# Another order for the last two front steps and for the middle steps of a two-layer vision tower

## The chip, the cores and the metric

The kernel runs on one core of a Trainium2 chip. The metric is device time in microseconds, from one launch to its end; the median of several runs counts. The engines are TensorE (PE in the profile, its weight loads PEld), VectorE (DVE), ScalarE (ACT), GpSimd (POOL) and SyncE (SP). They run side by side, each with its own queue in order, and wait for each other by semaphores. An engine also waits for its own earlier instruction by a semaphore where it reads that one's result.

## The reference

128 images are cut into 64 patches each, embedded, given a class token and multiplied by a positional table: 128 x 65 tokens of width 128. Two layers follow. L0 has attention (softmax over the queries) and 32 experts with a ReLU, two per token, gated by sigmoids; L1 mixes tokens by a decaying sum whose size is scaled by a norm, and has 16 experts with a GELU and four times the width, two per token, gated by softmax values.

```python
    h = _L0_tok_ref(x, ...)
    h = h + _L0_attn_ref(_layernorm(h, axis=-1), ...)
    h = h + _L0_ffn_ref(_layernorm(h, axis=-1), ...)
    h = h + _L1_attn_ref(_layernorm(h, axis=-1), L1_attn_k)
    h = h + _L1_ffn_ref(_layernorm(h, axis=-1), ...)
```

## The kernel before

**Front.** 16 groups of 8 images (520 tokens, five tiles of 104 rows). Each group is embedded, goes through attention (stages a1 to a4: token-major copy and norm, transposes, queries and keys, values and scores, softmax; b1 and b2: product with the values, sum h1T, transposes back to token-major htok), and is routed to the experts (r1 to r3). For each token and each of its two experts, a row of 132 numbers (the normalized token, place, gate, spread, mean) is scattered to the expert's list in HBM: POOL issues ten indirect DMAs per group (send). Where a row goes (slots) is the expert's base plus the token's rank there; the ranks come from one-hot rows (oh, ohs) by matmuls on PE (r3) and a running count.

A step works on the routing of group g and the attention of group g + 1. The last two steps, late_step on PE and ACT and a list of calls on DVE, belong to groups 14 and 15. There the router works on the sums h1T ahead of the norm (late_r2, with selC, the centred expert matrix), since the order of the logits doesn't change by the norm's scale: late_choice takes the two best, late_experts finds their indices and one-hots, late_added sums them, late_rows computes the norm's power (three dependent Newton instructions), the scaled logits eg, and writes the first copy of the rows; ACT copies them for the second expert (r1_rows1) and takes the exponential of eg; late_gate and late_slots end it. For group 15 the softmax and the product with the values are done in two halves of four images (last_a4 and last_b1 on DVE, last_b1 on PE).

**Tables and blocks of L0.** tables(L0) on DVE and PE computes from the counts which expert each block of 256 rows belongs to. Its first value, t_fr, says where each list ends; SP and ACT wait for it and write rows of padding there. 73 blocks follow: load the expert's weights and rows (SP, ACT), transpose, two matmuls with a ReLU between them, scale by the gate, scatter the results (POOL, two indirect DMAs a block). The first eight blocks are loaded before, from the groups that are known; the others wait for all rows and the padding.

**Middle.** 13 groups of 640 tokens. For each, two results per token are added (gather on DVE, line L2139), normed, mixed by two banded products on PE (delta, context), added to the tokens (mixed_in, L2178), normed, routed and sent (POOL, ten indirect DMAs a group; the send's issue is line L2316, that of the results L2344). Groups 0 and 1 lie among L0's blocks; groups 2 to 12 are steps of their own, mid_step on PE, ACT and DVE. Rows and slots have three buffers: group g may write its rows when the send of group g - 3 has landed (scattered). The names of the row buffers are rows (two of them) and w_emb (groups 2, 5, 8, 11).

**Blocks of L1** are like L0's, with four times the width; the results are added up and stored.

The order on each engine is written out by hand: a function per engine lists the calls, and a wait on one engine holds up all that stands behind it there. SP has no part in the change; POOL's queue is the sends and results in their order, unchanged.

## Time and profile before

| | |
|---|---|
| median of 3 runs | 1103.01 us (1102.77 to 1104.39) |
| profiled execution, its own time | 1099.68 us |
| its span, from the first to the last instruction | 1097.9 us |
| busy in the span: PE, DVE | 913.5 us (83%), 861.2 us (78%) |
| busy in the span: POOL, ACT | 676.5 us (62%), 498.8 us (45%) |
| front until L0's first table value | 448 us |
| L0's blocks, with groups 0 and 1 of the middle among them | to about 677 us |
| middle groups 2 to 12, and L1's tables | to about 816 us |
| L1's blocks and the sums | to the end |

The shares are means over stages that have different limits; what a change is worth is read in its stage.

### The profile page before, as it was taken

How to read it: one execution, taken by the hardware profiler on the slowest of the kernel's cores; microseconds unless marked ns; L12 is line 12 of the kernel's file. 1: busy time of each engine (PE TensorE's matmuls, PEld its weight loads, DVE VectorE, ACT ScalarE, POOL GpSimd, SP SyncE). 2: the span in 40 equal slices, each digit the busy share in tenths (PEclk: the TensorE clock that was granted, in tenths of full speed). 3: DMA queues.
4: the chain of work that ended last, by engine and by line, in shares of the span. 5: the costliest groups of instructions: out<-in, count | busy, mean ns of one | idle time of the engine just before them, and what ended most of it. 6: DMA issues, size and time to landing. Idle time of an engine off the chain costs nothing.

```text
span 1097.9 us, 21730 instructions
## 1 busy us (share of the span) xinstructions
PE 913.5 (83%) x6064; PEld 773.1 (70%) x6064; DVE 861.2 (78%) x3321; ACT 498.8 (45%) x1338; POOL 676.5 (62%) x622
## 2 busy tenths in 40 slices
PE   6999999999999996476775877767549999999992
PEld 2576666777766665366665866766549999999992
DVE  1488989888888986666686898998767777888883
ACT  1355555555544442111111554666525555655651
POOL 1026666767766646677677667777777555555553
PEclk9999999999999996678788887777759999999996
DMA  9955666555666204477779964665295888979886
GB/s 371 358 201 206 214 225 219 197 200 201 218 223 213 72 22 139 127 212 207 205 225 312 299 228 150 232 211 168 76 330 169 294 271 288 296 261 333 303 275 232
DMA packets 118664, 246.57 MB, mean 225 GB/s; under 512 B 20914, under 2 KB 85936, under 8 KB 112400
## 3 DMA queue, kind: packets, MB, share of 16 engines
q1 hardware_dynamic: 77440, 191.26, 51.5%
q0 software_dynamic: 18592, 34.68, 9.3%
q10 hardware_dynamic: 22512, 19.25, 5.8%
q8 instruction: 48, 0.79, 0.3%
q14 instruction: 72, 0.59, 0.2%
HBM read 201.68 MB, written 45.43 MB: 225 GB/s over the span
## 4 chain that ended last, share of the span: by engine, by line
PE 38%; DVE 25%; issue 11%; DMA 9%; SPq 7%; ACT 5%; POOL 3%; ACTq 1%; DVEq 0%; POOLq 0%
PE ps L1002 8%; PE ps L980 5%; DMA xin<-lists_L 4%; PE ps L753 3%; PE ps L820 3%; DMA results_L<-xin 3%; PE ps L804 2%; SPq L607 2%; POOL lists_L L2316 2%; SPq L609 2%; SPq L600 2%; ACT x_hi L1180 2%; PE ps L792 2%; PE ps L746 2%; DVE idx L1686 2%
## 5 line engine op out<-in xcount | busy, mean ns | idle before, releaser
L2316 POOL DMA_INDIRECT lists_L<-rows,slots x250 | 282.3, 1129 | 164.1 <-issue 156.1
L2344 POOL DMA_INDIRECT results_L<-xin x145 | 145.8, 1005 | 105.3 <-DVE xin L2116 73.7
L2344 POOL DMA_INDIRECT results_L<-xin,place x146 | 143.7, 984 | 59.7 <-issue 38.9
L753 PE MATMUL ps<-xin,w_emb 128*128 128x512 f32 x292 | 137.4, 607 | 10.1 <-DMA w_emb<-in_w_main 8.2
L1002 PE MATMUL ps<-xin,QK 128*128 128x128 f32 x838 | 115.6, 289 | 1.8 <-DVE xin L2116 1.7
L1002 PEld LDWEIGHTS ps<-xin,QK 128*128 128x128 f32 x838 | 108.2, 205 | 3.1 <-issue 3.0
L1364 ACT ACTIVATE QK<-ps,xin 128x256 f32<-128x256 f32 x164 | 64.2, 474 | 82.0 <-PE ps L980 82.0
L2325 POOL TENSOR_TENSOR x_lo<-xin,x_hi 128x2048 fp32r<-128x2048 f32 x13 | 60.1, 4626 | 63.3 <-ACT x_hi L1188 63.0
L957 PE MATMUL ps<-ident,xin 128*128 128x128 f32 x291 | 66.5, 311 | 36.0 <-DMA xin<-lists_L 33.8
L753 PEld LDWEIGHTS ps<-xin,w_emb 128*128 128x128 f32 x292 | 52.8, 194 | 58.8 <-issue 47.8
L2090 DVE TENSOR_SCALAR xin<-xin 128x128 f32<-128x128 f32 x291 | 92.9, 364 | 0.6
L1002 PE MATMUL ps<-xin,UH 128*128 128x128 f32 x648 | 89.1, 283 | 2.6 <-DVE xin L2116 2.4
L1207 ACT ACTIVATE h0T<-ps 128x256 f32<-128x256 f32 x73 | 27.8, 382 | 131.4 <-PE ps L957 100.7
L1002 PEld LDWEIGHTS ps<-xin,UH 128*128 128x128 f32 x648 | 81.4, 197 | 4.3 <-issue 4.3
L980 PE MATMUL ps<-x_hi,x_lo 128*128 128x256 f32 x256 | 78.6, 307 | 1.1 <-DVE x_lo L2084 1.1
L975 PE MATMUL ps<-h0T,xin 128*128 128x128 f32 (+1 forms) x326 | 59.5, 319 | 19.1 <-ACT h0T L1207 8.8
L980 PE MATMUL ps<-x_hi 128*128 128x256 f32 x256 | 73.1, 285 | 0.0
L980 PE MATMUL ps<-x_lo,x_hi 128*128 128x256 f32 x256 | 73.0, 285 | 0.0
L957 PEld LDWEIGHTS ps<-ident,xin 128*128 128x128 f32 x291 | 39.4, 158 | 43.8 <-DMA xin<-lists_L 41.3
L1364 ACT ACTIVATE UH<-ps,xin 128x256 f32<-128x256 f32 (+1 forms) x160 | 55.4, 429 | 31.1 <-PE ps L980 29.3
L975 PEld LDWEIGHTS ps<-h0T,xin 128*128 128x128 f32 x326 | 53.7, 237 | 21.7 <-ACT h0T L1207 11.2
L2105 DVE TENSOR_TENSOR xin<-ps,xin 128x256 f32<-128x256 f32 x81 | 32.1, 397 | 44.3 <-PE ps L1002 44.2
(347 smaller groups left out, 2418.8 us busy)
## 6 DMA issues: line engine op xcount, KB each, us to landing
xin<-in_x_main SPq DMA_DIRECT2D x48, 1536.0 KB, 6.7
xin<-in_w_L SPq DMA_DIRECT2D x81, 578.0 KB
xin<-in_w_L SPq DMA_DIRECT2D x98, 128.0 KB
xin<-lists_L SPq DMA_DIRECT2D x64, 132.0 KB
xin<-in_w_L ACTq DMA_DIRECT2D x65, 128.0 KB
x_hi<-results_L SPq DMA_DIRECT2D x13, 640.0 KB, 6.3
xin<-in_difference SPq DMA_DIRECT2D x13, 640.0 KB, 4.6
xin<-in_distance SPq DMA_DIRECT2D x13, 640.0 KB
```

What stands on the lines that cost most here:

```text
L753: mm = pe.matmul(psE[h], w_emb[:, k, :], xin[h][c][:, n, :], start=(k == 0), stop=False, skip_group_check=True)
L820: mm = pe.matmul(pair[2][:, c:c + SEQ], V[h][:, i, :], Pr[h][:, i, :], start=True, stop=True)
L957: mm = pe.transpose(ps[:, banks(l, i)[0], q * 128:(q + 1) * 128], xblk[b][:, q, 0:D], ident[:, :])
L975: mm = pe.matmul(bank_h(i, f)[:, of_part], w1, xTb[p2][:, of_part], start=True, stop=True)
L980: mm = pe.matmul(bank_h(i, f)[:, 0:n_in], w[p2][:, cols_f], x[p2][:, 0:n_in], start=(n2 == 0), stop=(n2 == 2), skip_group_check=True)
L1002: mm = pe.matmul(o, hTb[p2][:, f, rows_in], w2[:, f * D:(f + 1) * D], start=(f == 0), stop=(f == l.FC - 1))
L1364: ins = act.activation(hTb[p2][:, f, 0:n_in], ps[:, 2 + 2 * p2 + f // 2, f % 2 * l.block:f % 2 * l.block + n_in], ACT.Gelu, bias=b1)
L2090: ins = dve.tensor_scalar(xblk[u][:, q, 0:D], xblk[u][:, q, 0:D], xblk[u][:, q, SPREAD:SPREAD + 1], xblk[u][:, q, MEAN:MEAN + 1], ALU.mult ...
L2105: dve.tensor_tensor(yblk[u][:, 0:Q, :], y, wblk[u][:, None, l.W - D:l.W].to_broadcast([128, Q, D]), ALU.add)\
L2316: pool.indirect_dma_start(out=lists[l.name], out_offset=bass.IndirectOffsetOnAxis(ap=slots_of(l, g, h)[:, t, k:k + 1], axis=0), in_=buf[:, ...
L2325: pool.tensor_tensor(x_lo0[:, :, :].rearrange("p k n -> p (k n)"), xin[h][0][:, 0:KS, :].rearrange("p k n -> p (k n)"), x_hi0[:, :, :].rea ...
L2344: pool.indirect_dma_start(out=results[l.name], out_offset=bass.IndirectOffsetOnAxis(ap=where, axis=0), in_=yblk[u][:, q, :], in_offset=Non ...
```

## The change

In the last two front steps: ACT copies the transposed tokens of group 15 ahead of the guess for group 14's norm. PE computes the scores ahead of the values (last_a4 on PE), and DVE takes the scores (a3) ahead of the ranks and of the copy of the values, with the slots of group 14 between the two halves of the softmax. For group 15 PE transposes the sums (last_b2) ahead of the router (late_r2); DVE takes the statistics first, computes the power before the experts' indices, and no longer writes rows: ACT writes both copies from htok with a scale and a shift (last_rows; last_shift on DVE gives the shift). late_rows is split into late_power and late_rows, late_slots into late_pick and late_slots.

In the middle steps DVE's functions are written anew so that instructions that don't depend on each other alternate: the Newton steps of the next group's norm stand among the one-hots (newton_half, newton_off, newton_power), those of the mixing among the rows (mid_rows), the slots of the group before behind the first tile of the rows (mid_slots), the mean and variance of the next group between the logits and their maxima. ACT normalizes the next tokens before it copies the rows, and takes the gate's exponentials before the decays. The instructions are the same ones as before, but for the order and two additional waits.

```diff
+            def last_a4(g, h):
+
+                pe.wait_ge(q_ready, g + 1)
+                pe.wait_ge(k_ready, g + 1)
+                for i in range(GI):
+                    c = i // 4 * BANK + i % 4 * SEQ
+                    mm = pe.matmul(pair[1][0:SEQ, c:c + SEQ], KTt[:, i * SEQ:(i + 1) * SEQ],
+                                   QT[:, i * SEQ:(i + 1) * SEQ], start=True, stop=True)
+                mm.then_inc(s_ps, 1)
+                for i in range(GI):
+                    mm = pe.matmul(pair[0][0:SEQ, i * D:(i + 1) * D], x1T[h][:, i * SEQ:(i + 1) * SEQ], wv[:, :],
+                                   start=True, stop=True)
+                mm.then_inc(v_ps, 1)
+
+            def last_b2(g):
+
+                pe.wait_ge(h1T_ready, g + 1)
+                for t in range(TILES):
+                    if t == 2:
+                        pe.wait_ge(h1T_ready, g + 2)
+                    mm = pe.transpose(pair[2][0:ROWS, t * 128:(t + 1) * 128], h1T[:, t * ROWS:(t + 1) * ROWS], ident[:, :])
+                mm.then_inc(hT_ps, 1)
+
             def late_r2(g):
 
                 pe.wait_ge(h1T_ready, g + 1)
                 pe.wait_ge(consts_dve, 3)
                 for t in range(TILES):
-                    if t == 2 and g + 1 == GROUPS:
-                        pe.wait_ge(h1T_ready, g + 2)
                     mm = pe.matmul(late_logit[:, t, :], h1T[:, t * ROWS:(t + 1) * ROWS], selC[:, :], start=True, stop=True)
                 mm.then_inc(S["L0"].lg_ps, 1)
 
...
                 if g + 1 < GROUPS:
                     b1(g, h, j)
                     a1(g + 1, 1 - h, j + h)
+                    late_r2(g)
+                    b2(g, h, j)
                 else:
                     last_b1(g, h)
-                late_r2(g)
-                b2(g, h, j)
+                    last_b2(g)
+                    late_r2(g)
                 if g + 1 < GROUPS:
                     a2(g + 1, 1 - h, j + h)
                     a3(g + 1, 1 - h, j + h)
                 r3(L0, g, h, j)
                 if g + 1 < GROUPS:
-                    a4(g + 1, 1 - h, j + h)
+                    last_a4(g + 1, 1 - h)
 
...
+            def last_rows(g, h, j):
+
+                s, ln, buf = S["L0"], second["L0"], rows_of(L0, g, h)
+                act.wait_ge(s.top_ready, g + 1)
+                act.wait_ge(s.scattered[h], 16 * TILES * TOP * j)
+                for t in range(TILES):
+                    ins = act.activation(buf[:, t, :, 0:D], htok[h][:, t, None, :].to_broadcast([ROWS, TOP, D]), ACT.Identity,
+                                         scale=ln.rs[:, t:t + 1], bias=ln.shift[:, t:t + 1])
+                ins.then_inc(s.rows1_ready, 1)
+
...
@@ -1314,14 +1347,17 @@
                     a1(g + 1, o, jo)
                     guess(LNA, g + 1, statsA, logA, guessA)
                 b2(g, h, j)
+                if g + 1 < GROUPS:
+                    a2(g + 1, o, jo)
                 guessB(L0, g)
                 if g + 1 < GROUPS:
-                    a2(g + 1, o, jo)
                     a3(g + 1, o, jo)
                 late_r2(g)
-                r1_rows1(L0, g, h, j)
                 if g + 1 < GROUPS:
+                    r1_rows1(L0, g, h, j)
                     a4(g + 1, o, jo)
+                else:
+                    last_rows(g, h, j)
 
...
                     absolute(g + 1)
+                if 0 <= g + 2 < MG:
+                    normalized(g + 2)
                 if g >= 0:
                     r1_rows1(L1, g, g % 2, g // 2)
-                if 0 <= g + 2 < MG:
-                    normalized(g + 2)
                 if 0 <= g + 1 < MG:
                     guessB(L1, g + 1)
+                if g >= 0:
+                    r2(L1, g, g % 2, g // 2)
                 if 0 <= g + 2 < MG:
                     decays(g + 2)
-                if g >= 0:
-                    r2(L1, g, g % 2, g // 2)
                 if 0 <= g + 2 < MG:
...
-            def last_a4(g, h):
-
-                st = Steps(NA * g + 4)
...
+            def last_a4(g, h, n):
+
+                st, i = last_steps, slice(n * GI // 2, (n + 1) * GI // 2)
+                dve.wait_ge(exp_ready, g + 2 + n)
...
+                dve.tensor_tensor(Pr[h][:, i, :], Pr[h][:, i, :], ssum[:, i, None].to_broadcast([SEQ, GI // 2, SEQ]),
+                                  ALU.mult).then_inc(p_ready, 1)
+
+            last_steps = Steps(NA * (GROUPS - 1) + 4)
 
...
-            def late_rows(g, h, j):
-
-                s, w, ln, buf = S["L0"], W["L0"], second["L0"], rows_of(L0, g, h)
+            def late_power(g):
+
+                s, w, ln = S["L0"], W["L0"], second["L0"]
                 dve.wait_ge(s.guessB, g + 1)
                 dve.scalar_tensor_tensor(ln.half[:, 0, :], ln.guess[:, 0, :], -0.5, ln.guess[:, 0, :],
                                          ALU.mult, ALU.mult).then_inc(s.dveR, F.one())
@@ -1931,10 +1967,23 @@
                 dve.scalar_tensor_tensor(ln.rs, ln.off[:, 0, :], 1.5, ln.guess[:, 0, :],
                                          ALU.add, ALU.mult).then_inc(s.dveR, F.one())
                 dve.wait_ge(s.dveR, F.all())
+                if g + 1 == GROUPS:
+                    last_shift()
                 dve.tensor_tensor(w.eg[:, :, :], w.top8[:, :, 0:TOP], ln.rs[:, :, None].to_broadcast([L0.rows, TILES, TOP]),
                                   ALU.mult).then_inc(s.top_ready, 1)
+
+            def last_shift():
+
+                ln = second["L0"]
+                dve.wait_ge(S["L0"].dveR, F.all())
+                dve.scalar_tensor_tensor(ln.shift[:, :], ln.mv[:, :, 0], -1.0, ln.rs, ALU.mult, ALU.mult)
+
+            def late_rows(g, h, j):
+
+                s, ln, buf = S["L0"], second["L0"], rows_of(L0, g, h)
                 dve.wait_ge(s.scattered[h], 16 * TILES * TOP * j)
-                norm_apply(ln, htok[h], lambda t: buf[:, t, 0, 0:D]).then_inc(s.rows0_ready, 1)
+                if g + 1 < GROUPS:
+                    norm_apply(ln, htok[h], lambda t: buf[:, t, 0, 0:D]).then_inc(s.rows0_ready, 1)
                 dve.tensor_copy(buf[:, :, 0, MEAN], ln.mv[:, :, 0])
                 dve.scalar_tensor_tensor(buf[:, :, 0, SPREAD], ln.mv[:, :, 1], EPS, ln.rs, ALU.add, ALU.mult)\
                     .then_inc(s.spread_ready, 1)
...
-            def late_slots(g, h, j):
+            def late_pick(g):
 
                 s, w, p, E = S["L0"], W["L0"], L0.rows, L0.E
                 dve.wait_ge(s.rank_ps, g + 1)
@@ -1961,6 +2010,10 @@
                 dve.wait_ge(s.dveR, marks["added"])
                 dve.tensor_tensor(counted(L0, g + 1), counted(L0, g), w.added[:, 0:E], ALU.add).then_inc(s.dveR, F.one())
                 marks["counted"] = F.all()
+
+            def late_slots(g, h, j):
+
+                s, w, p, E = S["L0"], W["L0"], L0.rows, L0.E
                 dve.wait_ge(s.rank_read, g + 1)
...
             late_experts(g)
             r1(L0, g, h, j)
             late_added(g)
+            late_power(g)
             late_rows(g, h, j)
             late_gate(g, h)
+            a3(g + 1, 1, j)
+            late_pick(g)
+            a2(g + 1, 1, j)
+            last_a4(g + 1, 1, 0)
             late_slots(g, h, j)
-            a2(g + 1, 1, j)
-            a3(g + 1, 1, j)
-            last_a4(g + 1, 1)
+            last_a4(g + 1, 1, 1)
             g, h = 2 * j + 1, 1
             last_b1(g, h)
+            r1(L0, g, h, j)
             late_choice(g)
+            late_power(g)
             late_experts(g)
-            r1(L0, g, h, j)
+            late_rows(g, h, j)
             late_added(g)
+            late_gate(g, h)
+            late_pick(g)
             late_slots(g, h, j)
-            late_rows(g, h, j)
-            late_gate(g, h)
 
...
+            def mid_slots(g):
+                s, w = S["L1"], W["L1"]
+                dve.wait_ge(s.dveR, marks["rank"])
+                dve.scalar_tensor_tensor(slots_of(L1, g, g % 2)[:, :, :], w.idx8[:, :, 0:TOP], float(L1.room),
+                                         w.rank[:, :, :], ALU.mult, ALU.add).then_inc(s.slot_ready, 1)
+
+            def mid_rows(g):
+
+                s, ln, x, buf = S["L1"], second["L1"], m_tok[g % 2], rows_of(L1, g, g % 2)
+                norm, magnitude, turn = one_of(g + 2), one_of(g + 1), g + 3
+                which = slice(0 if norm is not None else 1, 2 if magnitude is not None else 1)
+                dve.wait_ge(s.dveR, marks["power"])
+                dve.wait_ge(s.scattered[g % 3], 16 * TILES * TOP * (g // 3))
+                for t in range(TILES):
+                    ins = dve.tensor_scalar(buf[:, t, 0, 0:D], x[:, t, :], ln.mv[:, t, 0:1], ln.rs[:, t:t + 1],
+                                            ALU.subtract, ALU.mult)
+                    if t == 0 and g > LAST + 1:
+                        mid_slots(g - 1)
+                    if t == 2 and magnitude is not None:
+                        dve.wait_ge(m_guess, turn)
+                        dve.scalar_tensor_tensor(LNC.half[:, which, :], LNC.guess[:, which, :], -0.5,
+                                                 LNC.guess[:, which, :], ALU.mult, ALU.mult).then_inc(dveM, sm.one())
+                    if t == 3 and magnitude is not None:
+                        dve.wait_ge(dveM, sm.all())
+                        dve.scalar_tensor_tensor(LNC.off[:, which, :], LNC.base[:, which, :], TINY,
+                                                 LNC.half[:, which, :], ALU.add, ALU.mult).then_inc(dveM, sm.one())
+                ins.then_inc(s.rows0_ready, 1)
+                if magnitude is not None:
+                    dve.wait_ge(dveM, sm.all())
+                    if norm is not None:
+                        dve.wait_ge(m_ntok, norm)
+                    dve.wait_ge(actx_ready, magnitude)
+                    dve.scalar_tensor_tensor(LNC.power[:, which, :], LNC.off[:, which, :], 1.5,
+                                             LNC.guess[:, which, :], ALU.add, ALU.mult).then_inc(dveM, sm.one())
+                dve.tensor_copy(buf[:, :, 0, MEAN], ln.mv[:, :, 0])
+                dve.scalar_tensor_tensor(buf[:, :, 0, SPREAD], ln.mv[:, :, 1], EPS, ln.rs, ALU.add, ALU.mult)\
+                    .then_inc(s.spread_ready, 1)
+                if magnitude is not None:
+                    dve.wait_ge(dveM, sm.all())
+                    if norm is not None:
+                        dve.scalar_tensor_tensor(LNC.shift[:, :], LNC.mv[:, :, 0], -1.0, LNC.rs, ALU.mult, ALU.mult)
+                    dve.tensor_tensor(mag, ssq, LNC.power[:, 1, :], ALU.mult).then_inc(m_powers, 1)
+                dve.tensor_copy(buf[:, :, :, PLACE].bitcast(I32),
+                                places["L1"][:, g:g + 1, :].rearrange("p o (t k) -> p (o t) k", t=TILES))\
+                    .then_inc(s.place_ready, 1)
+
+            def mid_tokens(g):
+
+                s, ln = S["L1"], second["L1"]
+                if g + 3 < MG:
+                    h = (g + 3) % 2
+                    dve.wait_ge(m_in[h], 16 * ((g + 3) // 2 + 1))
+                    h2 = h2tok[(g + 3) % 3]
+                    dve.tensor_tensor(h2[:, :, :], yin[h][:, :, 0, :], yin[h][:, :, 1, :], ALU.add).then_inc(m_free[h], 1)
...
+                if g + 1 < MG:
+                    mixed_in(g + 1)
...
+                if g + 1 < MG:
+                    dve.wait_ge(s.htok_ready, g + 2)
+                    for t in range(TILES):
+                        ins = dve.bn_stats(ln.bn[:, t, :], m_tok[(g + 1) % 2][:, t, :])
+                    ins.then_inc(s.statsB_step, 1)
...
+            def mid_ranked(g):
+
+                s, w, E, p = S["L1"], W["L1"], L1.E, L1.rows
+                if g + 1 < MG:
+                    newton_half(g + 1)
...
             def mid_step(g):
 
-                h, j = g % 2, g // 2
-                r1_apply(L1, g, h, j)
+                mid_rows(g)
                 if g == L1.known + 1:
                     first_table(L1)
-                if g < MG - 1:
-                    powers(one_of(g + 2), one_of(g + 1), g + 3)
-                if g + 3 < MG:
-                    gather(g + 3)
-                if g + 1 < MG:
-                    mixed_in(g + 1)
-                    r1(L1, g + 1, 1 - h, (g + 1) // 2)
+                mid_tokens(g)
                 if g == L1.known:
                     first_counts(L1)
-                st = r2(L1, g, h, j)
-                r2_gate(L1, g, h, j, st)
...
+                mid_chosen(g)
+                mid_ranked(g)
...
+            for f in (newton_half, newton_off, newton_power):
+                f(LAST + 1)
             for g in range(LAST + 1, MG):
                 mid_step(g)
+            mid_slots(MG - 1)
+            dve.wait_ge(S["L1"].slot_ready, MG)
             tables(L1)
```

mid_chosen is r2's part up to the indices, and mid_ranked the rest of r2, r2_gate, r3 and r3_slots, in the alternating order; newton_half, newton_off and newton_power are newton's three instructions.

## Rows read from the trace of the kernel before

**Rows 1.** DVE's timeline, 425 to 448: start us, us, engine, line, operation, output<-inputs.
```profile
429.78 0.75 DVE L1606 SCALAR_TENSOR_TENSOR Sm<-ps,causal 65x260 f32<-65x260 f32 x2
430.56 0.69 DVE L1610 TENSOR_REDUCE smax<-Sm 65x8 f32<-65x520 f32 x1
...
434.54 0.42 DVE L1865 TENSOR_TENSOR Pr<-Pr,ssum 65x260 f32<-65x260 f32 x1
...
437.50 0.43 DVE L1880 TENSOR_TENSOR UH<-UH,ps 128x260 f32<-128x260 f32 x1 [1.18 <-PE ps L854]
439.27 0.33 DVE L1887 COPY lg<-ps 104x160 f32<-104x160 f32 x1 [1.34 <-PE ps L865]
...
442.02 0.24 DVE L1911 TENSOR_TENSOR ohs<-oh 104x160 bf16<-104x160 bf16 x1
...
443.38 0.45 DVE L1553 BATCH_NORM_AGGREGATE mvB<-bnB 104x2 f32<-104x6 f32 x5
...
445.14 0.17 DVE L1973 SCALAR_TENSOR_TENSOR slots<-idx,rank 104x10 uint32<-104x10 uint32 x1
...
446.04 1.36 DVE L1558 TENSOR_SCALAR rows<-htok,mvB,powerB 104x128 f32<-104x128 f32 x5
...
447.87 0.12 DVE L1782 SCALAR_TENSOR_TENSOR t_fr<-iotaB,ps 1x32 int32<-1x32 f32 x1
```

**Rows 2.** POOL's timeline, 440 to 452; in brackets the idle time before.
```profile
449.07 0.99 POOL L2316 DMA_INDIRECT lists_L<-rows,slots  x1 [6.15 <-ACT rows L1207]
```

**Rows 3.** Chain of waits, 395 to 650: start us, us, what.
```profile
464.83 2.06 DMA lists_L<-padrows
```

**Rows 4.** DVE's timeline, 680 to 700: slots of group 2.
```profile
682.97 0.17 DVE L1739 SCALAR_TENSOR_TENSOR slots<-idx,rank 128x10 uint32<-128x10 uint32 x1
```

**Rows 5.** POOL's timeline, 684 to 838, first issue of group 2 and first result of L1.
```profile
690.95 0.96 POOL L2316 DMA_INDIRECT lists_L<-w_emb,slots  x1 [0.30 <-issue]
...
832.45 0.99 POOL L2344 DMA_INDIRECT results_L<-xin  x1 [0.30 <-issue]
```

**Rows 6.** Busy time by stretches; columns: PE, PEld, DVE, ACT, POOL busy, PEclk, DMA, GB/s.
```profile
815.00:822.00 7.00, 5.92 (x32) 5.46 (x28) 3.65 (x11) 1.75 (x5) 5.43 (x6) 0.50 0.94 290
...
846.00:1098.00 252.00, 227.87 (x1983) 226.48 (x1983) 190.31 (x533) 134.87 (x347) 135.07 (x135) 0.97 0.83 282
```

**Rows 7.** PE's timeline, 844 to 847.
```profile
846.68 0.33 PE L957 MATMUL ps<-ident,xin 128*128 128x128 f32 x1 [1.58 <-DMA xin<-lists_L]
```

**Rows 8.** PE's timeline, 412 to 448.
```profile
418.09 1.13 PE L777 MATMUL ps<-ident,ntok 104*128 104x104 f32 x5 [2.00 <-DVE ntok L1558]
422.40 2.10 PE L792 MATMUL ps<-XT,small 128*128 128x260 f32 x4 [3.18 <-ACT XT L1207]
...
426.36 1.91 PE L804 MATMUL ps<-small,XT 128*65 128x128 f32 x16
428.11 1.11 PE L810 MATMUL ps<-QK 128*65 128x65 f32 x16
433.82 3.65 PE L854 MATMUL ps<-Pr,V 65*128 65x65 f32 x16 [4.60 <-DVE Pr L1865]
```

**Rows 9.** ACT's timeline, 412 to 448.
```profile
421.76 0.58 ACT L1207 ACTIVATE XT<-ps 128x520 f32<-128x520 f32 x1
...
440.37 0.70 ACT L1207 ACTIVATE htok<-ps 104x640 f32<-104x640 f32 x1 [6.32 <-PE ps L770]
```

**Rows 10.** DVE's timeline, 795 to 811: rows of group 12, L1's first table value.
```profile
798.96 1.37 DVE L1558 TENSOR_SCALAR rows<-htok,mvD,powerD 128x128 f32<-128x128 f32 x5
...
809.95 0.16 DVE L1782 SCALAR_TENSOR_TENSOR t_fr<-iotaB,ps 1x16 int32<-1x16 f32 x1 [0.51 <-PE ps L894]
```

**Rows 11.** POOL's timeline, 584 to 796: first and last of the delayed issues.
```profile
587.02 1.17 POOL L2344 DMA_INDIRECT results_L<-xin,place  x1 [0.30 <-issue]
...
791.73 1.38 POOL L2316 DMA_INDIRECT lists_L<-rows,slots  x1 [0.30 <-issue]
```

**Rows 12.** DVE's timeline, 784 to 796: the add at the last of them.
```profile
791.45 0.83 DVE L2178 TENSOR_TENSOR htok<-atok,xin 128x640 f32<-128x640 f32 x1 [1.46 <-ACT xin L1437]
```

121 lines of the change are left out of this document (107 added, 14 removed).

## The prediction

> **What bounds the kernel now.** I first read the page's busy time by slices against the stretches of the program, then the chain of waits over the change's first place (400 to 470 us), then the timelines of VectorE (DVE), ScalarE (ACT), TensorE (PE) and GpSimd (POOL) there, and last POOL's timeline through the middle. The reader is to see three stages with different limits.
>
> At the end of the front (groups 14 and 15) almost nothing overlaps: the chain hops PE, ACT, DVE, PE. It ends in the first table value t_fr at 447.87 and in the sends of group 15 at 449.07 [rows 1, 2]. Everything behind hangs on t_fr: the pad rows that ACT and SP write after it have landed at 466.9 [rows 3], and the loads of the ninth block on wait for them.
>
> In the middle (groups 2 to 12 of L1) the chain of waits names DVE for every step up to 798, and DVE has hardly a gap. I don't follow it there. The tile names on POOL's issues tell which group is being sent, since groups 2, 5, 8, 11 send from w_emb. The slots of group 2 are ready at 683.14, but its first issue is at 690.95, and POOL goes from there to the first L1 result at 832.45 with gaps of 0.30 only [rows 4, 5]: 110 issues in 141.5 us, 1.286 each. POOL is always behind DVE and sets the end of the middle; the releaser "DVE slots" that the trace prints is a coincidence of times.
>
> In L1's blocks PE is busy 228 of 252 us [rows 6]. Their start is one wait: PE had finished what it could and sat 1.58 us until a token load landed at 846.68 [rows 7]. That load waits for a result scatter, which stands behind POOL's last send.
>
> **The change part by part.** *ACT's copy of x1T ahead of guessB (step 14).* The transposes end at 419.22 (418.09 + 1.13), the copy began at 421.76 because the guess stood before it [rows 8, 9]. It can start at 419.3: 2.5 us earlier. The guess waits for statistics that come only after that, so putting it second costs nothing; were they early, it would be late by the copy, 0.58.
>
> *Scores before values, DVE's a3 before pick and copy of V.* q and k (from 419.9 in place of 422.40) end at 423.7, k's copy at 424.4; then the scores, 1.11 as before or up to twice that if the clock is low, to 425.5 to 426.1. Sm and smax take 1.47 (429.78 to 431.25), so smax ends at 427.6 instead of 431.25: 3.65 earlier [rows 1, 8]. From there ACT's eight exponentials end after 2.8; DVE has pick, V's copy, the first half of the probabilities and the rest of the slots in that time, 3.5 in all, and then the second half: 4.4 from smax to the end of Pr against 3.7 before (431.25 to 434.96). Gain left 2.95. The product with V starts on the first half: its 3.65 [rows 8] run from 430.3 with little wait between the halves, to 433.95, and h1T ends at 434.4 instead of 437.93 [rows 1]: **3.5 us**. What it costs: slots of group 14 come 2.4 later, so POOL's ten sends end at 445.2 and not at 442.92; POOL sat idle 6.15 us there [rows 2], so 3.9 of idle time is left as cover, and group 15 can go at 445.2.
>
> *Transposes before the router, rows of group 15 by ACT.* Before, h1T to t_fr was 9.94 (437.93 to 447.87). After: three transposes that wait for the second half 0.7 (five take 1.13 at 418.09), htok's copy 0.70, statistics 1.57 (442.26 to 443.83); the router's result is there by then (behind the transposes' new wait stand only the router and the ranks, which need the same half). Logits to ohs 2.99 (439.27 to 442.26); between them the power and eg 0.73 (445.31 to 446.04) and one new small instruction, shift, 0.2; copies and gate 0.47 (447.40 to 447.87); added, pick, slots 1.48 (443.83 to 445.31); then PE's counts, which lay under the rows before and are now a wait, 0.51 as in the other table [rows 1, 8, 9, 10]. Sum 9.35; I add 0.2 for waits: **0.4 us**. The row writing of 1.36 leaves DVE. On ACT it is five instructions of 2x128 columns; the trace has no such shape; by the 0.70 for 640 columns [rows 9] they take between 1.4 (columns alone) and 3.5 (five whole ones); I take 2. DVE's 4 us from eg to the last slot hides either; without that cover the difference would be added to POOL's start only.
>
> So t_fr comes 3.9 earlier, group 15's sends 3.9 earlier. The pads, tables and blocks of L0 follow by the same instructions, and POOL's unbroken run (which begins in L0's last blocks) with them. **-3.9 us**, bounds -2.0 (PE at the low clock through V's product, so that everything from V's copy comes late) and -4.7.
>
> *Middle steps.* The Newton links, means and slots are set between independent instructions; DVE's step gets shorter. I cost this at **nothing**: POOL's issues hide it, and the third row buffer stops DVE when it runs ahead. Rows of group 12 were written at 798.96; they need group 9's send, whose last issue ended at 793.11 [rows 10, 11], so DVE can gain less than 5.8 there, and I take 3.5. If POOL were not the bound, the saving would be about 1.5 per step. Slots now wait behind the next group's buffer wait; two sends earlier must have landed, while POOL has a whole send of 12.9 us left: no starvation.
>
> *POOL against DVE.* An add of two 640-column tiles (L2139, L2178) that is running when an issue starts delays it: the add of 791.45 to 792.28 made the issue at 791.73 last 1.38 and not 0.97 [rows 11, 12]. In the steady steps each add starts just after an issue has begun, and none costs. Where steps are uneven (thirteen adds, from the issue at 587.02 to the one at 791.73) five issues lost 0.08 to 0.41, 1.18 in all, 0.09 per add [rows 11]. The new order breaks the steady places. Eighteen adds are in groups 2 to 11; two cost 0.55 before. Bounds: 0 and 18 x 0.41 = 7.4 in place of 0.55. I take the drifting rate: 1.6, **+1.1 us**.
> The Trainium skill (SBUF — State Buffer, section "Who interferes with whom") says that a VectorE instruction with two SBUF inputs contends with a GpSimd instruction that reads SBUF, and that the second to issue fully blocks; these rows agree. The same section holds that descriptor generation is not stalled by a tensor_tensor; by that the term would be 0 and the sum -3.9, but the 1.38 speaks against it.
>
> *PE's wait before 846.68.* L1's tables come 3.5 earlier than POOL's end, so PE's 1.58 us wait grows to about 5. That alone costs nothing, for the load sets the restart. But after the idle time before 815 PE ran 7 us at half of the full clock by its granted clock of 0.50 [rows 6]; the same here would add up to 3.5. PE works between two shorter waits, so I take 0, and keep 3.5.
>
> Sum: -3.9 + 0 + 1.1 + 0 = -2.8. The profiled execution took 1099.68 (span 1097.9, 1.8 around it), 3.3 below the median of the runs, 1103.01; against it 1096.9, against the median **1100.2 us**. Below, times are against the median.
>
> **Rivals.**
> *Given back (no change).* The front gains, but POOL's delays come to 2 to 5 us more, or PE restarts at half clock, or V's product meets the low clock: 1101 to 1105. For it: POOL has no slack from 650 to 832, so each delay counts whole; against: five of thirteen drifting adds cost anything.
> *Slower: port collisions alone.* The new order puts each add across the start of an issue, and keeps it there, since DVE is held by POOL's landings and so keeps step with it. At 0.41 for 18 adds, 7.4 less 0.55 is +6.9, net +3.0: 1106.0. It decides from 0.36 per add (6.0 + 0.55 over 18). For it: the place copy and the first add now stand side by side; against: no stretch of the trace shows more than one such delay in a step.
> *The chain is right about DVE.* Then nine steps give 1.5 each, 13.5, and with the front 17: about 1086. Against it stands the 7.8 us between slots and issue of group 2.
> *The front does nothing*, because pads and loads end by another wait: 1103. Against: the pads start from t_fr.
>
> **How the numbers follow.** About 0.2% (2.2 us) is what a measurement can tell. Forecast (front kept, POOL pays little): 0.46; given back: 0.35; a front that does nothing: 0.03; slower: 0.12; DVE the bound: 0.04. Faster 0.50, same 0.38, slower 0.12. The range reaches from the full front with no delays and some luck in PE's clock, -6.5, to the middle of the slower case, +1.5: 1096.5 to 1104.5; the likeliest case alone is 1098.3 to 1100.8.
>
> **What would show it.** In the new profile: x1T's copy right after its transposes; smax about 3.6 earlier; t_fr and group 15's first send near 444 and 445; five ACT instructions after eg that nothing waits for; the first mid send and the first L1 result earlier by the same 4, less long issues between; DVE with gaps in the middle; PE idle around 5 us before L1's ninth block. It is wrong if POOL has gaps in the middle (then DVE counted), if many issues last 1.2 or more (collisions), or if t_fr moves by less than 2.

## The result and the profile after

The changed kernel takes 1096.92 us (median of 4 runs, 1092.84 to 1098.53) against 1103.70 for the kernel before (4 runs, 1102.77 to 1104.83): 6.8 us less, a ratio of 0.9933 (95% interval 0.9903 to 0.9962). I had forecast 1100.2, range 1096.5 to 1104.5: the direction is right, the gain more than twice as large as its sum of 2.8. The profiled execution took 1092.84, span 1091.1; the pair of profiled executions also differs by 6.84.

VectorE's timeline of the kernel after, 424 to 445, for [rows 1] (start us, us, engine, line, operation, output<-inputs, idle time before):

```profile
425.47 0.76 DVE L1642 SCALAR_TENSOR_TENSOR Sm<-ps,causal 65x260 f32<-65x260 f32 x2 [0.76 <-PE ps L852]
426.27 0.69 DVE L1646 TENSOR_REDUCE smax<-Sm 65x8 f32<-65x520 f32 x1
...
427.44 1.21 DVE L1632 TENSOR_TENSOR V<-ps,per_row 65x1024 f32<-65x1024 f32 x1
...
429.83 0.17 DVE L2026 SCALAR_TENSOR_TENSOR slots<-idx,rank 104x10 uint32<-104x10 uint32 x1
...
430.44 0.42 DVE L1899 TENSOR_TENSOR Pr<-Pr,ssum 65x260 f32<-65x260 f32 x1
...
432.93 0.42 DVE L1916 TENSOR_TENSOR UH<-UH,ps 128x260 f32<-128x260 f32 x1 [0.99 <-PE ps L868]
435.06 1.06 DVE L1584 BATCH_NORM_STATS2 bnB<-htok 104x6 f32<-104x128 f32 x5 [1.71 <-ACT htok L1230]
...
442.28 0.17 DVE L2026 SCALAR_TENSOR_TENSOR slots<-idx,rank 104x10 uint32<-104x10 uint32 x1
442.97 0.18 DVE L1818 SCALAR_TENSOR_TENSOR t_fr<-iotaB,ps 1x32 int32<-1x32 f32 x1 [0.52 <-PE ps L915]
```

smax (the scores' maxima, for the softmax) ends at 426.96 and not at 431.25, the second half of the probabilities at 430.86 (434.96), h1T at 433.35 (437.93), and t_fr starts at 442.97 (447.87): 4.9 earlier. Three smaller groups of the same kernel: TensorE's timeline [rows 8], ScalarE's [rows 9], POOL's [rows 2].

```profile
424.31 1.13 PE L852 MATMUL ps<-QK 128*65 128x65 f32 x16 [0.24 <-ACT QK L1264]
425.27 1.91 PE L856 MATMUL ps<-small,XT 128*65 128x128 f32 x16
```

```profile
418.94 0.60 ACT L1230 ACTIVATE XT<-ps 128x520 f32<-128x520 f32 x1 [2.35 <-PE ps L777]
...
438.64 2.55 ACT L1334 ACTIVATE rows<-htok,shiftB,powerB 104x256 f32<-104x256 f32 x5
```

```profile
444.33 0.99 POOL L2543 DMA_INDIRECT lists_L<-rows,slots  x1 [0.30 <-issue]
...
686.38 0.97 POOL L2543 DMA_INDIRECT lists_L<-w_emb,slots  x1 [0.30 <-issue]
...
742.65 1.36 POOL L2543 DMA_INDIRECT lists_L<-rows,slots  x1 [0.30 <-issue]
...
827.63 0.99 POOL L2571 DMA_INDIRECT results_L<-xin  x1 [0.30 <-issue]
```

Behind t_fr the last pads go out 4.8 earlier too, by the chain of waits [rows 3]:

```profile
460.04 1.98 DMA lists_L<-padrows
```

ACT's copy of x1T follows its transposes; the five instructions for the rows take 2.55, and nothing waits for them. Group 15's first send comes 4.74 earlier and now directly behind group 14's ten. In the middle POOL is what it was: from group 2's first issue to the first result of L1 141.25, against 141.50 [rows 5], with no gap but its 0.30. So the first result of L1 comes 4.82 earlier, the last one 6.80 (1075.48 against 1082.28).

VectorE's waits of the kernel after, 690 to 800 (line, what it waited for: us in total, times, longest):

```profile
DVE halfC L2287 <- ACT guessC L1457: 7.2, 7, 1.5
DVE lg L2346 <- PE ps L838: 4.3, 1, 4.3
DVE pick L2407 <- PE ps L903: 3.7, 6, 0.8
DVE rows L2281 <- DMA lists_L<-rows,slots: 3.5, 3, 2.5
```

The new order did shorten VectorE's step (busy 78.3 of the 100 us from 695 to 795; before, 87.6), and the time came back as waits, among them the one for a row buffer to come free (the last line). TensorE begins L1's blocks at 807.18, and stands still twice, each time until a token load has landed:

```profile
835.54 0.44 PE L978 MATMUL ps<-ident,xin 128*128 128x128 f32 x2 [2.14 <-DMA xin<-lists_L]
...
840.98 0.33 PE L978 MATMUL ps<-ident,xin 128*128 128x128 f32 x1 [1.78 <-DMA xin<-lists_L]
```

These 3.92 in place of 1.58 [rows 7] cost nothing by the clock. Busy time by stretches (columns as in [rows 6]): 0.57 granted at the start of L1's blocks, 1.00 around those waits.

```profile
807.20:814.20 7.00, 5.92 (x32) 5.52 (x31) 3.66 (x11) 1.85 (x5) 5.37 (x6) 0.57 1.06 358
...
830.00:840.00 10.00, 7.06 (x60) 6.68 (x58) 6.68 (x18) 4.08 (x10) 7.65 (x8) 1.00 0.66 199
```

### The profile page after: what moved, and what is told of

Its sections match the earlier page's. It is cut to its first block, busy times and chain, and to the rows that moved or that the text cites. A ratio compares the mean times of both kernels' runs of the same rounds, so it can differ in the third digit from the quotient of the medians.

```text
span 1091.1 us, 21712 instructions
## 1 busy us (share of the span) xinstructions
PE 914.6 (84%) x6064; PEld 773.3 (71%) x6064; DVE 848.0 (78%) x3317; ACT 501.7 (46%) x1342; POOL 675.7 (62%) x622
## 4 chain that ended last, share of the span: by engine, by line
PE 42%; DVE 20%; issue 11%; DMA 9%; ACT 7%; SPq 6%; POOL 4%; ACTq 1%; DVEq 0%; POOLq 0%
PE ps L1023 9%; PE ps L1001 6%; PE ps L753 4%; POOL lists_L L2543 3%; DMA xin<-lists_L 3%; PE ps L820 3%; PE ps L804 2%; PE ps L1121 2%; SPq L607 2%; SPq L609 2%; DMA results_L<-xin 2%; PE ps L777 2%; ACT x_hi L1203 2%; SPq L600 2%; PE ps L792 2%
```

## The experiments

Single executions of one kernel differ by several us, so the stages are compared from mark to mark in POOL's and VectorE's timelines: group 13's first send (s13), t_fr, the first send of the middle (m0), the first and last result of L1 (r0, rZ). "Over 0.97" is what the longer ones of the 142 issues from m0 to r0 took beyond 0.97 us each, summed. One profile each, us:

| kernel | s13 to t_fr | t_fr to m0 | m0 to r0 | over 0.97 | r0 to rZ |
|---|---|---|---|---|---|
| before | 35.93 | 201.57 | 183.01 | 2.3 | 249.83 |
| before_again | 35.89 | 200.22 | 184.84 | 4.0 | 249.62 |
| the change | 30.78 | 201.33 | 183.33 | 2.5 | 247.85 |
| change_again | 31.09 | 203.30 | 183.98 | 3.1 | 249.98 |
| change_third | 31.14 | 200.38 | 183.04 | 2.2 | 248.57 |
| change_fourth | 31.17 | 201.60 | 183.86 | 3.0 | 251.19 |
| front_alone | 31.05 | 200.01 | 183.28 | 2.5 | 248.83 |
| front_alone_2 | 30.79 | 198.65 | 184.63 | 3.8 | 249.49 |
| middle_alone | 35.97 | 199.66 | 183.23 | 2.5 | 250.54 |
| middle_alone_2 | 35.55 | 200.06 | 184.58 | 3.5 | 250.49 |
| middle_alone_3 | 35.92 | 200.31 | 184.81 | 3.7 | 250.77 |
| attention_part | 31.61 | 200.10 | 184.43 | 3.7 | 252.79 |
| routing_part | 35.34 | 199.63 | 183.48 | 2.8 | 251.21 |
| copy_first | 33.80 | 201.18 | 183.16 | 2.1 | 249.96 |
| dve_more | 31.01 | 197.87 | 184.42 | 3.7 | 249.04 |
| two_inputs | 31.18 | 200.53 | 189.43 | 8.6 | 250.93 |
| pool_more | 31.11 | 201.19 | 194.13 | 4.2 | 251.13 |
| late_start | 31.13 | 201.44 | 184.70 | 3.9 | 249.80 |
| late_start_2 | 31.13 | 201.26 | 184.90 | 3.8 | 249.63 |
| ends_first | 29.95 | 200.47 | 183.50 | 2.7 | 247.86 |

**Which half gives the gain.** The kernel before with the front's edits alone, or the middle's alone:

```diff
 front_alone
+                    last_a4(g + 1, 1 - h)
...
+                    last_b2(g)
...
+                    last_rows(g, h, j)
...
+            a3(g + 1, 1, j)
+            late_pick(g)
 middle_alone
+                if 0 <= g + 2 < MG:
+                    normalized(g + 2)
...
+                mid_rows(g)
...
+                mid_chosen(g)
+                mid_ranked(g)
```

*change_again*

> The changed kernel once more, as a yardstick for its parts. Profile so far: L0's first table value 4.9 us earlier, the first result of L1 4.8 earlier, the end 6.8 earlier. Theory A (only the front counts, the last 2 us of the 6.8 are a matter of load waits in L1's blocks that differ from execution to execution): -4.9 to -6.8, and the first result of L1 again within 0.5 of 827.6. Theory B (the middle's order adds 2 us by an earlier start of L1's blocks): -6.8 again, with L1's transposes again about 8 us earlier than before.

*front_alone*

> Only the last two front steps are changed; the middle is as before. Theory A: t_fr near 443, the first result of L1 near 827.5, and the time that of the whole change, within 1 us (-6 to -7 against before). Theory B: the front gives only its 4.9 (about 1098.8), 2 short of the whole change, and L1's first transposes are 4.9 earlier, not 8. Theory C (DVE is the bound of the middle, as the chain of waits names it): -4.9 here too, and the rest comes from the middle.

*middle_alone*

> Only the middle steps are changed; the front is as before (t_fr near 447.9). Theory A: no change, within 1 us, first result of L1 within 0.7 of 832.45. Theory B: first result within 0.7 of 832.45 too, but L1's blocks start about 3 us earlier, and the end comes 2 earlier (about 1101.7). Theory C: -5 or more, first result of L1 earlier by that. Rival of my prediction (collisions): later by 1 or more, with issues over 1.1 us in the middle.

Measured: change_again 1095.43 against 1100.94, ratio 0.9945 (0.9924 to 0.9966); front_alone 1097.27, 0.9964 (0.9947 to 0.9982); middle_alone 1101.92, 1.0003 (0.9985 to 1.0022). The front's edits take 4.8 to 5.1 from s13 to t_fr, the middle's take nothing from m0 to r0. The first result comes no earlier by the middle's order (183.23 from m0 to r0), so theory C falls. A and B stay: 2.1 us lie between the front's ratio and the whole's. My absolute times ("827.6 within 0.5") missed, since executions start at either of two offsets: s13 lies at 411.8 to 412.4 or at 413.6 to 413.9, in kernels of both kinds. Hence the table.

**Who sets the middle's pace.** The whole change with work added to each of the eleven middle steps: two VectorE instructions with one input (dve_more) or two (two_inputs), or one instruction on POOL (pool_more). Nothing reads what they write; the waits that order these writes among themselves are left out here, and in late_start further down.

```diff
 dve_more
                 mid_rows(g)
+                for n in range(2):
+                    dve.tensor_scalar(V[0][:, 0:TILES, :], m_tok[g % 2][0:SEQ, :, :], 2.0, None, ALU.mult)
 two_inputs
                 mid_rows(g)
+                for n in range(2):
+                    dve.tensor_tensor(V[0][:, 0:TILES, :], m_tok[g % 2][0:SEQ, :, :], m_tok[g % 2][0:SEQ, :, :], ALU.add)
 pool_more
             for g in range(LAST + 1, MG):
+                pool.memset(scratch[:, 0:1024], 0.0)
                 send(L1, g, g % 2)
```

*dve_more*

> The whole change, and in each of the eleven middle steps VectorE does two more instructions of 640 columns with one input, to a tile that nothing reads: some 0.8 us each or less, 1 to 1.6 per step, 11 to 17 in all. Theories A and B (POOL's issues set the middle's pace): the first result of L1 stays within 1 us of 827.6; by B alone the end comes up to 2 later, as L1's blocks start later. Theory C: 11 to 17 later at the first result and at the end.

*pool_more*

> The whole change, and in each of the eleven middle steps POOL clears 1024 unused columns ahead of its ten sends, by the 0.32 us for 264 columns at the kernel's start about 1.0 us. If POOL's issues set the middle's pace: from group 2's first send to the first result of L1 141.3 plus eleven, or plus ten where the first lies ahead, 151 to 153, and the end 8 to 11 later (about 1105 to 1108 against the median before of 1101 to 1103). If DVE's chain sets it: under 145, and the end within 2 of the change's.

*two_inputs*

> Like the run with two more VectorE instructions per step, but they are adds with two SBUF inputs (0.83 us each). If only such adds delay POOL's issues, the 22 of them make 5 to 15 issues longer by up to 0.8 each: from group 2's first send to the first result of L1 143 to 148, against 141.9 with one input. If the delay comes from any VectorE work, or is rare by the steps' own rhythm: 142 again. If DVE's chain sets the middle's pace: 141.5 plus 15.

dve_more: 1096.62, ratio 0.9961 (0.9940 to 0.9981), 141.92 from group 2's first send to r0: eleven times 0.98 us of VectorE work vanish there. (In time it is 1.8 slower than change_again beside it, 0.9961 against 0.9945; the intervals overlap, and no stage of its profile shows it.) pool_more: 1106.98, 1.0043 (1.0021 to 1.0066), 151.68 there, 10.4 more than in the profile of the change. Ten of its clears lie behind that first send. Each takes 0.97 and leaves 0.17 of idle time in place of the 0.30, so it costs 0.84, 8.4 in all; the other 2.1 are long issues (3.4 over 0.97 on that way, 1.3 in the change). POOL sets the pace: less its long issues, the way from group 2's first send to r0 takes 139.8 to 139.9 in the kernel before, in the four profiles of the change, in dve_more and in two_inputs. two_inputs: 1101.70, 1.0011 (0.9993 to 1.0030), 147.28: the same place, 0.83 us each, and 5.4 more than dve_more, of which 5.3 are long issues. POOL's and VectorE's timelines of two_inputs show how:

```profile
720.04 1.34 POOL L2548 DMA_INDIRECT lists_L<-rows,slots  x1 [0.30 <-issue]
721.68 1.28 POOL L2548 DMA_INDIRECT lists_L<-rows,slots  x1 [0.31 <-issue]
...
733.45 2.31 POOL L2548 DMA_INDIRECT lists_L<-w_emb,slots  x1 [0.30 <-issue]
```

```profile
719.73 1.66 DVE L2427 TENSOR_TENSOR V<-htok 65x640 f32<-65x640 f32 x2
721.31 0.81 DVE L2322 TENSOR_TENSOR atok<-x_lo 128x640 f32<-128x640 f32 x1
...
732.52 1.66 DVE L2427 TENSOR_TENSOR V<-xin 65x640 f32<-65x640 f32 x2
734.10 0.81 DVE L2322 TENSOR_TENSOR ntok<-x_hi 128x640 f32<-128x640 f32 x1
```

The issue that begins at 733.45, among three adds in a row (732.52 to 734.91), ends at 735.76, 0.85 behind the last of them. So the rival "port collisions alone" has a real price, though the change does not pay it: adds laid over the starts of issues in each step take the whole gain away. Whether it is a port that the two engines wait for is not shown; that the issue waits for the add is.

**What the front is made of.** attention_part has only step 14's edits, routing_part only group 15's (both shown against front_alone); copy_first is the kernel before with ACT's two calls exchanged.

```diff
 attention_part
-                    last_b2(g)
-                    late_r2(g)
+                    late_r2(g)
+                    b2(g, h, j)
...
-                    last_rows(g, h, j)
...
 routing_part
-                    last_a4(g + 1, 1 - h)
+                    a4(g + 1, 1 - h, j + h)
...
-            a3(g + 1, 1, j)
             late_pick(g)
+            late_slots(g, h, j)
             a2(g + 1, 1, j)
+            a3(g + 1, 1, j)
...
 copy_first
                 b2(g, h, j)
+                if g + 1 < GROUPS:
+                    a2(g + 1, o, jo)
                 guessB(L0, g)
                 if g + 1 < GROUPS:
-                    a2(g + 1, o, jo)
                     a3(g + 1, o, jo)
```

*attention_part*

> Of the front's edits only those of step 14 (ACT's copy first, scores ahead of values, DVE's scores ahead of ranks and V); group 15 is routed as before, the middle is as before. Executions start up to 1.7 us apart, so the front is measured from the first send of group 13 to t_fr: 35.93 before, 30.78 and 31.09 with the change. My prediction (3.5 of 3.9 from this part): 32.4. By the profile of the change (h1T 4.6 earlier, of which 0.3 was given in ahead of it): 31.1 to 31.5. Rival (the parts help each other, as the transposes ahead of the router start on the early half): over 33.

*routing_part*

> Only group 15's routing is changed (transposes ahead of the router, rows by ACT, DVE's order); step 14 and the middle are as before. My prediction (0.4): 35.5 from group 13's first send to t_fr. By the profile of the change (h1T to t_fr 9.6 against 9.9): 35.6. Rival (the parts are not additive): under 34.5 or over 35.9.

*copy_first*

> The kernel before with one edit: ACT's copy of x1T ahead of the guess. My prediction gave this 2.5 us of start and the rest of the attention part's gain to the scores ahead of the values. If the copy's 2.5 go through to t_fr: 33.4 from group 13's first send to t_fr, of 35.93 before and 31.61 with the whole attention part. If VectorE, which takes ranks, slots and the copy of V ahead of the scores, holds it up: 34.5 or more, and the gain is mostly the scores' order.

attention_part: 1097.06, 0.9960 (0.9940 to 0.9979); routing_part: 1100.60, 0.9999 (0.9977 to 1.0021); copy_first: one run, 1098.17. From s13 to t_fr the copy takes 2.1, the rest of the attention part 2.2 more (31.61), the routing 0.5 on top (31.1). Alone, the routing is worth 0.3: from h1T to t_fr it is 9.93 to 9.94 in six profiles with the old routing (10.07 in attention_part) and 9.61 to 9.64 in the twelve with the new one, routing_part among them. The 0.6 of routing_part's 35.34 flatters it: in its execution, as in front_alone_2's, middle_alone_2's and that of the change shown above, the router's matmul of group 14 ran 1.34 to 1.48 and not 1.94, and t_fr came some 0.35 sooner. Busy time of the kernel after, of that stretch:

```profile
413.00:415.00 2.00, 1.70 (x12) 1.70 (x13) 1.85 (x12) 0.22 (x2) 1.39 (x3) 0.72 0.31 76
```

Of change_third, where it took 1.94:

```profile
413.00:415.00 2.00, 2.00 (x12) 2.00 (x13) 1.38 (x11) 0.47 (x2) 1.39 (x3) 0.50 0.43 115
```

The granted clock is at its lower level (0.50, 1.2 GHz) throughout in change_third, and at the full one for part of the stretch in the profile of the change; the two matmuls begin after the same idle time of 0.97 and 0.98 us. So 0.35 of the 5.15 in the profile of the change (30.78 against 35.93) belong to the execution, not to the edit.

The same holds for the two larger pieces of TensorE behind the router, the scores (L852) and the product with the values (L868). TensorE's timelines of change_third, then of front_alone, which has the same order here:

```profile
424.22 1.13 PE L852 MATMUL ps<-QK 128*65 128x65 f32 x16 [0.54 <-ACT QK L1264]
429.46 3.41 PE L868 MATMUL ps<-Pr,V 65*128 65x65 f32 x16 [2.36 <-DVE Pr L1899]
```

```profile
426.31 1.78 PE L852 MATMUL ps<-QK 128*65 128x65 f32 x16 [0.24 <-ACT QK L1264]
432.20 1.08 PE L868 MATMUL ps<-Pr,V 65*128 65x65 f32 x8 [2.35 <-DVE Pr L1899]
433.57 1.11 PE L868 MATMUL ps<-Pr,V 65*128 65x65 f32 x8 [0.30 <-DVE Pr L1899]
```

Busy time of these stretches, in the same order:

```profile
424.20:425.40 1.20, 1.18 (x18) 1.20 (x19) 0.40 (x3) 0.60 (x1) 0.59 (x1) 1.00 0.75 167
429.40:432.90 3.50, 3.44 (x18) 3.44 (x18) 2.28 (x7) 0.28 (x2) 1.63 (x2) 0.55 0.41 115
```

```profile
426.30:428.10 1.80, 1.79 (x18) 1.80 (x19) 0.48 (x2) 0.59 (x1) 0.29 (x1) 0.61 0.61 143
432.20:434.70 2.50, 2.20 (x17) 1.96 (x18) 2.22 (x7) 0.21 (x2) 1.00 (x1) 0.97 0.33 87
```

In change_third the scores have the full clock (1.00) and the product is mostly at the lower level (0.55); in front_alone, as in ends_first, it is the other way round (0.61, then 0.97). h1T ends alike, 21.50 and 21.43 after s13: either way the low clock is paid for once.

**The size, again.**

*before_again*

> The kernel before once more, unchanged, for the spread of single executions. If the differences between executions that I ascribe to noise are that: 35.9 within 0.1 from group 13's first send to t_fr, but 198 to 203 from t_fr to the first send of the middle (201.57 before), 183 to 184 from there to the first result of L1, 248 to 252 from there to the last. If instead the change shortens L0's blocks too: 201.5 within 0.5 here.

*change_third*

> The changed kernel a third time. If the gain is the front's 5.0, POOL's delays no more than before, and a matter of half a microsecond at the start of L1's blocks: -5 to -6. If the 6.8 of the first measurement is the size and the middle adds 2: -6.5 to -7. t_fr 30.8 to 31.1 after group 13's first send in either case.

*middle_alone_2*

> The middle's order alone, again, for its sign: the whole change measured 6.1 to 6.8 faster three times, the front alone 4.0 (2.0 to 5.8), the middle alone 0.3 slower (1.6 faster to 2.4 slower). If L1's blocks gain from their start 3 us earlier: 1 to 2 faster. If the middle is worth nothing, as I predicted: within 0.7 of before.

*middle_alone_3*

> The same kernel once more, so that the two together tell 1.5 from nothing: the same two numbers.

*front_alone_2*

> The front alone, again. If the front is the whole gain: 5 to 6.5 faster, as the change. If the middle adds 1 to 2: 4 to 5 faster, and from the first result of L1 to the last one 250 to 251 (249 with the middle's order).

*late_start*

> The whole change, and ahead of L1's tables VectorE does seven instructions of 0.49 us that nothing reads, so that L1's blocks start 3.4 later against POOL, as they do in the kernel before (17.4 ahead of the first result in place of 20.5). If the earlier start is worth 1 to 2 us: 4 to 5 faster than before. If it is worth nothing, as the ninth block waits for POOL's last send: 6 to 6.8, as the change.

*change_fourth*

> The changed kernel a fourth time, beside its version with the late start of L1's blocks. If the gain over the front's 4.8 is spread between executions: anywhere from -4.5 to -7. If it is real: -6 to -7.

*late_start_2*

> The change with seven idle VectorE instructions ahead of L1's tables, again. If the earlier start of L1's blocks is worth 1.5: 1 to 2 us slower than the change in the same call. If it is worth nothing: within 0.7 of it.

```diff
 late_start
             dve.wait_ge(S["L1"].slot_ready, MG)
+            for n in range(7):
+                dve.tensor_scalar(V[0][:, 0:TILES, :], m_tok[0][0:SEQ, :, :], 2.0, None, ALU.mult)
             tables(L1)
```

before_again took 1102.12. Ratios: change_third 0.9940 (0.9919 to 0.9962), change_fourth 0.9950 (0.9933 to 0.9967), front_alone_2 0.9948 (0.9927 to 0.9968), middle_alone_2 1.0016 (0.9996 to 1.0035), middle_alone_3 0.9981 (0.9965 to 0.9997), late_start 0.9957 (0.9941 to 0.9973), late_start_2 0.9960 (0.9944 to 0.9976). One less the ratio, times the median before: the change gains 7.4 (6.8 by the medians), 6.1, 6.6 and 5.5 us, the front alone 4.0 and 5.7, the middle alone -0.3, -1.8 and 2.1, the change with the late start 4.7 and 4.4. The middle is worth nothing on the mean of three; but middle_alone_2 and 3 are the same kernel, measured side by side, and differ by 3.9, so 1.5 us can't be told from such a spread. The expectations don't settle it either: change_third fell where a middle worth 2 would put it, front_alone_2 where the front is the whole gain, and the two late_start runs where an earlier start is worth 1 to 2. before_again missed in one mark: 184.84 from m0 to r0, not 183 to 184, by its long issues (4.0).

late_start_2 is 1.1 slower than change_fourth beside it (0.9960 against 0.9950), and the intervals overlap. Its seven instructions moved the start of L1's blocks less than the 3.4 that was meant: 19.0 ahead of r0, 19.1 in late_start, 20.5 to 21.5 in the four profiles of the change. The stretch that differs from change_fourth is m0 to r0, by 1.0, in long issues: those behind the start of L1's blocks took 1.0 over 0.97 each, summed, in late_start_2, 1.2 in late_start and in before_again (also 19.0 ahead), 0.3 in change_fourth. The start alone does not fix that sum: middle_alone_2 and middle_alone_3 start 21.8 and 21.6 ahead and have 1.4 and 0.4. A lead of TensorE (theory B) shows nowhere: the three profiles of the middle alone start 21.6 to 21.8 ahead and take 250.5 to 250.8 from r0 to rZ, the kernel before starts 17.4 and 19.0 ahead and takes 249.8 and 249.6.

**One more step in the same direction.** ends_first adds up group 15's counts right behind the one-hots' sums and computes t_fr ahead of the slots; PE's counts for it wait for the table of counts and no longer for the slots. Only VectorE's list of calls is shown.

```diff
             late_added(g)
+            late_counted(g)
             late_gate(g, h)
+            late_known(g)
             late_pick(g)
+            list_ends(L0)
             late_slots(g, h, j)
             tables(L0)
```

*ends_first*

> The whole change, and for group 15 VectorE adds up the counts right after the one-hots' sums, and computes t_fr between the picked ranks and the slots, so that TensorE's counts lie beside other work: t_fr 1.0 to 1.2 earlier, 29.7 to 29.9 after group 13's first send, group 15's first send 0.1 to 0.3 later. If the pads set the ninth block's load, as the chain names them: its first load 1 us earlier against group 13's first send. If group 15's sends set it: no earlier. In time either is at the edge of what can be told: 0 to -1.2 against the change.

t_fr comes 1.2 earlier (29.95), group 15's first send 0.9 later (33.27 after s13, 32.4 in the change), and SP's first load behind the pads 1.2 earlier than in change_third beside it (461.63 - 411.98 = 49.65 against 462.68 - 411.84 = 50.84): the pads set it, as the chain says. The 0.9 is not the edit's: front_alone, with the change's order there, has 33.35, and in both the scores ran slowly (1.75 and 1.78). In time it is 0.9948 (0.9927 to 0.9969), the change 0.9940 beside it: 1 us more is not to be seen in the total, and I don't claim it as a better kernel.

## Why the prediction was right in direction and short in size

*What bounds it: right.* POOL sets the middle (pool_more, dve_more), t_fr sets what follows the front, and TensorE's longer wait ahead of L1's ninth block cost nothing (clock 1.00). The releaser in the chain of waits that named VectorE was, as I took it, a coincidence.

*The front, -3.9: the step that failed, by size.* Marked from s13, the change's usual execution has t_fr at 31.1; I had forecast 32.0 (444 less 411.94). The miss is in scores ahead of values, the "3.5 us" up to h1T: I had h1T end at 434.4, 22.46 after s13, and it ended at 21.4 to 21.6 in every profile with both parts and a slow router, 4.5 earlier than before and not 3.5. My sum paid for the low clock twice. The scores, "1.11 as before or up to twice that if the clock is low", I took from the late end (426.1), and V's product at 3.65, which it took before at the lower level throughout (granted 0.50). No profile shows both. In change_third the scores took 1.13, so smax ended 15.04 after s13, against my 15.66, and V's product took 3.41; in front_alone the scores took 1.78 and smax ended at 15.91, later than I had it, but V's product took 2.48 with its wait between the halves. A smaller part is VectorE under the exponentials, "3.5 in all": from smax's end to the start of the second half it was 3.07 or 3.08 in every profile with both parts, so 3.9 and not 4.4 to the end of the probabilities, and the product's second half could start sooner. Together 0.96 at h1T in change_third. The last leg, h1T to t_fr, was right: 9.6 against 9.55, with ACT's rows at 2.55 (I took 2) hidden as supposed. With these the front is -4.8.

*POOL against VectorE, +1.1: the other step that failed.* "I take the drifting rate": new order, new drift, more delays. In the profile of the change eleven of the 20 adds from 648 to 786 do cross the start of an issue, but six of them with their last 0.11 us or less, and those issues lasted 0.97. The other five made issues last 1.08 to 1.39; four of them belong to the eighteen adds that I had counted, and cost 0.98 where I took 1.6 (0.55 before). So it is +0.4 in this pair of profiles, and nothing on the mean: over 0.97 the seven profiles of the change and of the middle alone have 2.2 to 3.7 (mean 2.9), the seven with the middle's old order 2.1 to 4.0 (mean 3.0). I read a rate out of one execution, and the kernel before alone varies by 1.7 in that sum (2.3 and 4.0). The mechanism is there: two_inputs reached 5.4.

*Middle, 0: right.* Its three runs are on both sides of nothing.

*Sum.* -4.8 + 0 + 0 + 0 = -4.8 against the -2.8 that I gave; the two mis-sized terms make up the 2.0. The 6.8 of the first measurement holds a further 2.0 that neither term explains. The four measurements of the change lie 0.7 to 2.6 beyond -4.8. No stage shows this: with the two profiles before and four after, t_fr to m0 is 200.9 and 201.7, m0 to r0 183.9 and 183.6, r0 to rZ 249.7 and 249.4, and the 2.0 gained there in the first pair of profiles (249.83 against 247.85) is gone in the mean. Whether a further microsecond is real stays open; its cause was not found, and that it comes from the middle's order alone is not supported by its three runs.

## What to carry to other kernels

Before a stage is credited with a gain, ask which queue never stops there; here POOL's issues, 0.30 apart, told that nine shortened VectorE steps would be worth nothing. When executions of one kernel differ by more than the effect, measure from mark to mark in the traces: here two executions agreed within 0.1 us from a send to a table value when the router's matmul ran alike, while totals differed by 7. Where one uncertain thing, here TensorE's clock, stands in two terms of a sum, don't take its dearer end in both: that took about 1 of the 4.8 away. And a rate read from a handful of events in one execution is no better than its spread between executions.

## What the hardware showed

- Launches have two offsets 1.7 us apart, already there at the first send (80.6 or 82.2), in kernels of both kinds.
- From m0 to r0 nearly all that differs between executions is delayed issues: the stretch less its "over 0.97" is 180.7 to 181.1 in all the profiles but pool_more's, which has the clears in it.
- An indirect issue that begins under a VectorE add with two SBUF inputs ends about 0.85 us behind it, also behind three adds in a row (2.31 us). In the profiles other than two_inputs', from 560 to 800, 136 issues began with more than 0.15 us of such an add still to run, and every one ended 0.83 to 0.87 behind it; 229 others had an add begin 0.15 to 0.5 us into them, and lasted 0.96 to 0.99. So it is the start of an issue that waits, and an add that comes later costs it nothing. The Trainium skill (SBUF — State Buffer, section "Who interferes with whom") has such an add contend with reads of GpSimd, and infers that descriptor generation escapes. The runs agree with that for the later part of an issue, and not for its start: with two inputs the middle became 5.4 us longer than with one. What an issue does in its start is not shown.
- L0's blocks, from t_fr to m0, took 197.9 to 203.3 us with the same instructions. What makes the difference was not looked into.
